# Four-layer attention kernel, one core: gated layers may start beside the layer that shares their memory, order of steps replaced

## Time and profile before

| | |
|---|---|
| median of 3 runs | 2008.59 us |
| the profiled execution | 2009.47 us, its span from first to last instruction 2007.7 us |
| PE, share of the span | 98% |
| DVE | 74% |
| ACT | 58% |
| POOL | 35% |
| DMA | 104.5 MB, mean 52 GB/s |
| TensorE's granted clock | full in all 40 slices |

### The profile page before, as it was taken

The page is one execution under the profiler, slowest core; times in us unless marked ns, Lnnn a source line. Parts: engine busy times, 40 slices in busy tenths (PEclk is TensorE's granted clock), DMA queues, the critical chain, the costliest instruction groups (busy, mean ns, idle before and its releaser), DMA issues.

```text
span 2007.7 us, 41814 instructions
## 1 busy us (share of the span) xinstructions
PE 1960.4 (98%) x15876; PEld 1257.5 (63%) x15876; DVE 1491.6 (74%) x4779; ACT 1155.5 (58%) x2602; POOL 711.1 (35%) x897
## 2 busy tenths in 40 slices
PE   8999999999999999999999999999999999999997
PEld 6666655666665666656666566755666566676566
DVE  8986667766878768868779687796787966856535
ACT  1554765575637766376644757367573676627642
POOL 6322325242433333333324334234153342313321
PEclk9999999999999999999999999999999999999999
DMA  4001211111211121112211112111120111202200
GB/s 171 2 2 43 71 64 61 56 64 35 69 33 50 64 59 46 55 36 74 59 38 45 54 56 63 39 59 54 46 70 30 62 54 39 66 27 72 71 16 7
DMA packets 33381, 104.52 MB, mean 52 GB/s; under 512 B 3360, under 2 KB 13728, under 8 KB 33056
## 3 DMA queue, kind: packets, MB, share of 16 engines
q1 hardware_dynamic: 30880, 99.76, 15.1%
q0 software_dynamic: 2304, 2.10, 0.9%
HBM read 95.56 MB, written 6.29 MB: 51 GB/s over the span
## 4 chain that ended last, share of the span: by engine, by line
PE 66%; DVE 21%; ACT 7%; issue 2%; POOL 1%; ACTq 0%; DVEq 0%; POOLq 0%
PE ps L981 18%; PE ps L1773 9%; PE ps L1755 9%; PE ps L1763 8%; PE ps L1527 6%; DVE probs L1474 4%; DVE ps L1374 3%; PE ps L1715 3%; PE ps L1624 3%; ACT PTc L1226 3%; PE ps L1703 3%; PE ps L1610 3%; PE ps L1681 2%; PE ps L1586 2%; ACT probs L1270 2%
## 5 line engine op out<-in xcount | busy, mean ns | idle before, releaser
L1162 POOL TENSOR_SCALAR probs<-probs,rtotal 128x512 f32<-128x512 f32 x512 | 347.6, 698 | 538.7 <-DVE rtotal L1483 538.1
L1270 ACT ACTIVATE probs<-probs,peak 128x512 f32<-128x512 f32 x512 | 365.0, 714 | 184.6 <-DVE peak L1479 184.0
L1474 DVE CUSTOM_DVE_ANT_0 probs<-ps,band 128x512 f32<-128x512 f32 x512 | 332.6, 687 | 79.3 <-PE ps L1755 78.9
L1279 ACT ACTIVATE PT<-ps 128x512 f32<-128x512 f32 x512 | 265.2, 620 | 24.7 <-PE ps L1763 24.7
L1763 PE MATMUL ps<-ident,probs 128*128 128x128 f32 x2048 | 250.7, 275 | 1.6 <-POOL probs L1162 1.4
L1763 PEld LDWEIGHTS ps<-ident,probs 128*128 128x128 f32 x2048 | 225.3, 141 | 42.7 <-issue 28.5
L1374 DVE CUSTOM_DVE_ANT_0 ps<-ps,later 128x512 f32<-128x512 f32 (+3 forms) x512 | 233.2, 527 | 17.1 <-PE ps L1586 16.1
L1755 PE MATMUL ps<-KT,QT 64*128 64x512 f32 x1024 | 242.9, 606 | 1.0 <-DVE QT L1463 0.6
L1773 PE MATMUL ps<-PT,Vb 128*64 128x512 f32 x1024 | 238.5, 601 | 0.0
L981 PE MATMUL ps<-xnT,wb 128*128 128x512 f32 x512 | 235.5, 600 | 0.9 <-ACT xnT L1189 0.6
L1226 ACT ACTIVATE PTc<-ps 128x384 f32<-128x384 f32 (+1 forms) x384 | 168.1, 550 | 62.4 <-PE ps L1610 61.2
(11 more groups left out here) (166 smaller groups left out, 3277.3 us busy)
## 6 DMA issues: line engine op xcount, KB each, us to landing
band<-in_band SPq DMA_DIRECT2D x64, 896.0 KB, 4.6
wb<-in_w_b SPq DMA_DIRECT2D x64, 384.0 KB, 3.1
x<-in_x SPq DMA_DIRECT2D x16, 256.0 KB, 3.7
out<-x SPq DMA_DIRECT2D x16, 256.0 KB, 2.1
cos<-in_cos SPq DMA_DIRECT2D x8, 256.0 KB, 2.6
sin<-in_sin SPq DMA_DIRECT2D x8, 256.0 KB, 2.9
wob<-in_wo_b SPq DMA_DIRECT2D x1, 1024.0 KB, 9.1
wqk<-in_wqk_a SPq DMA_DIRECT2D x1, 512.0 KB, 6.0
```

What stands on the lines that cost most here:

```text
L1162: last = g.tensor_scalar(unit, unit, rtotal[:, r % 8, e:e + 1], 1.0, ALU.mult, ALU.mult)
L1270: last = a.activation(unit, unit, ACT.Exp, bias=peak[:, r % 8, e:e + 1], accum_out=total[:, r % 8, e:e + 1])
L1279: a.activation(PT[:, k % 2, e, :, tile_of(q)], bank(now, name).rearrange("p (k n) -> p k n", k=NT), ACT.Copy).then_inc(act_read, 1)
L1474: v.tensor_tensor_reduce(out=probs[:, (r + LENT) % ROWS_HELD, e, :], in0=bank(now, name), in1=band[:, k % 2, e, lo:lo + T], scale=1.0, sca ...
```

## The change

Four things change.

1. In `whole()` the two gated layers no longer follow the whole layer ahead in their home. `held_back` adds conditions to single steps instead. Layer 3 of s-1 may start `f_ln` after the causal layer's last `c_p2`; its `f_part` and `f_gather` still wait for `c_y`. Layer 1 of s+1 may start `f_ln` after layer 3's last `f_p2`; `f_part` follows layer 3's last `f_vb`, `f_rank` its last `f_va`, `f_gather` and `f_spread` its `f_add`. In the last pass (s = 7) the old rule stands.
2. The early phase's tiles move inside the home to places that are free by then: `logit_junk`, `gate_row`, `above`, `tie` over `gHI` and `gLO`, `xn_lo` over the second half of `PTf`; in layer 3 one more set, `gated_last`, lies over the causal layer's `HI`.
3. Semaphore waits that this needs are added: on DVE ahead of the logits (for `c_p2` or `f_p2`), on ACT in `f_part` of layer 3 (for `c_y`), on POOL in `f_part` of layer 1 (for `f_vb`).
4. Every value of `PLACE` is replaced, in all 210 rows of the table; `CYCLE` and the costs in `WORK` stay.

No operation of the computation is added or left out.

```diff
-    ("cycle", "c_y"): [-896, -3188],
...
-    ("cycle", "f_ln"): [-120],
...
-    ("cycle3", "f_add"): [5190],
...
-    ("cycle3", "f_ln"): [2230],
...
-    ("cycle3", "f_sc"): [5404],
...
+    ("cycle", "c_y"): [-920, -2849],
...
+    ("cycle", "f_ln"): [-238],
...
+    ("cycle3", "f_add"): [5413],
...
+    ("cycle3", "f_ln"): [4142],
...
+    ("cycle3", "f_sc"): [5796],
...
+def held_back(layer, behind):
+
+    return [(x, a, b + behind.get(x.kind, [])) for x, a, b in layer]
...
-            side = add(ffn_steps(s - 1, 3), left, turned + side)
+            if turned:
+                last_p2 = [Step("c_p2", s + 1, 0, 3, 2)]
+                side = add(held_back(ffn_steps(s - 1, 3), {"f_part": turned, "f_gather": turned, "f_turn": turned}), left, last_p2)
+            else:
+                side = add(ffn_steps(s - 1, 3), left, side)
             if s + 1 < B:
-                side = add(ffn_steps(s + 1, 1), turned, side)
+                done = {"f_part": [Step("f_vb", s - 1, 3, 1)], "f_rank": [Step("f_va", s - 1, 3, 1)],
+                        "f_gather": side, "f_spread": side}
+                side = add(held_back(ffn_steps(s + 1, 1), done), turned, [Step("f_p2", s - 1, 3, 3)])
...
-                         part("xn_lo", 1024, [P, NT, D], F32R), part("pick", 3072, [P, NT, CAP], F32R),
-                         part("logit_junk", 4096, [P, NT, D]), part("gate_row", 5120, [P, T]),
+                         part("xn_lo", 5120, [P, NT, D], F32R), part("pick", 3072, [P, NT, CAP], F32R),
+                         part("logit_junk", 1024, [P, NT, D]), part("gate_row", 1024, [P, T]),
...
+                                if l == 1 and s >= 2:
+                                    at_least(pool, dve_full, plan.unit(Step("f_vb", s - 2, 3, 1), now))
...
+                            if l == 3 and s + 2 < B:
+                                at_least(act, dve_full, plan.unit(Step("c_y", s + 2, 0, 1), now))
...
+                            if kind == "f_ln" and l == 3 and s + 2 < B:
+                                at_least(dve, act_full, last_unit(Step("c_p2", s + 2, 0, 3, 2), now))
+                            if kind == "f_ln" and l == 1 and s >= 2:
+                                at_least(dve, act_full, last_unit(Step("f_p2", s - 2, 3, 3), now))
```

More of the change, by code:

```diff
@@ L314 @@
[L314 to L327, removed]
@@ L328 @@
[L328 to L341, removed]
@@ L397 @@
-    ("last1", "f_hk"): [16566],
-    ("last1", "f_hm"): [12587, 16487],
-    ("last1", "f_idx"): [28848],
-    ("last1", "f_k"): [16502],
-    ("last1", "f_ln"): [29156],
-    ("last1", "f_m"): [15479, 24859],
-    ("last1", "f_mk"): [13382],
-    ("last1", "f_p1"): [13899, 13347, 15820, 13912],
-    ("last1", "f_p2"): [14402, 16479, 15277, 15555],
-    ("last1", "f_part"): [15919],
-    ("last1", "f_q"): [24858],
-    ("last1", "f_rank"): [15078],
-    ("last1", "f_row"): [13349],
-    ("last1", "f_rq"): [29156],
@@ L426 @@
-    ("last2", "f_p1"): [20538, 19976, 20663, 20764],
-    ("last2", "f_p2"): [20786, 20935, 20608, 20468],
-    ("last2", "f_part"): [18279],
-    ("last2", "f_q"): [20057],
-    ("last2", "f_rank"): [20308],
-    ("last2", "f_row"): [20165],
-    ("last2", "f_rq"): [-859],
-    ("last2", "f_sc"): [23696],
-    ("last2", "f_v"): [20786],
-    ("last2", "f_va"): [21047, 21532],
-    ("last2", "f_vb"): [15227, 17058],
-    ("last2", "f_xq"): [20405],
+    ("cycle", "b_k"): [823, 329, 785, 911, 1209, 1703, 2405, 2804],
@@ new lines @@
+    ("cycle", "f_k"): [195],
+    ("cycle", "f_ln"): [-238],
+    ("cycle", "f_m"): [320, 364],
+    ("cycle", "f_o"): [612],
+    ("cycle", "f_p1"): [272, 273, 299, 327],
+    ("cycle", "f_p2"): [344, 357, 272, -226],
+    ("cycle", "f_part"): [-356],
+    ("cycle", "f_q"): [198],
+    ("cycle", "f_rank"): [77],
+    ("cycle", "f_row"): [-30],
+    ("cycle", "f_rq"): [231],
+    ("cycle", "f_spread"): [225],
+    ("cycle", "f_v"): [271],
+    ("cycle", "f_va"): [406, 546],
+    ("cycle", "f_vb"): [152, -630],
@@ new lines @@
+    ("cycle3", "f_part"): [3793],
+    ("cycle3", "f_q"): [5082],
+    ("cycle3", "f_rank"): [4832],
+    ("cycle3", "f_row"): [4569],
+    ("cycle3", "f_rq"): [3074],
+    ("cycle3", "f_sc"): [5796],
+    ("cycle3", "f_v"): [5085],
+    ("cycle3", "f_va"): [5505, 5635],
+    ("cycle3", "f_vb"): [5095, 5471],
+    ("cycle3", "f_xq"): [3583],
+    ("first", "b_k"): [-499, 948, -411, 218, 1567, 2212, 3083, 2202],
+    ("first", "b_ln"): [2790],
+    ("first", "b_nrm"): [1568, 1572, 622, 1089, 206, 1709, 698, 377, 1317, 1576, 2189, 2190, 2222, 2188, 1994, 2216,
+        3004, 1566, 923, -1603, 3029, 215, 1361, 2270, 1466, 2531, 2638, 2332, 329, 2199, 3415, 3302],
@@ new lines @@
+    ("first0", "c_xq"): [-10, 355],
+    ("first0", "c_xt"): [8233],
+    ("first0", "c_y"): [902, -1196],
+    ("first0", "f_gate"): [344],
+    ("first0", "f_gather"): [1165],
+    ("first0", "f_hk"): [155],
+    ("first0", "f_hm"): [-200, 1237],
+    ("first0", "f_k"): [330],
+    ("first0", "f_ln"): [603],
+    ("first0", "f_m"): [1241, 1460],
+    ("first0", "f_o"): [1498],
+    ("first0", "f_p1"): [1221, 1171, 1282, 1238],
+    ("first0", "f_p2"): [-201, 1369, -1220, 493],
+    ("first0", "f_part"): [987],
@@ new lines @@
+    ("first0", "f_q"): [15],
+    ("first0", "f_rank"): [1071],
+    ("first0", "f_row"): [971],
+    ("first0", "f_rq"): [270],
+    ("first0", "f_spread"): [1370],
+    ("first0", "f_v"): [332],
+    ("first0", "f_va"): [1461, 1232],
+    ("first0", "f_vb"): [-212, -336],
+    ("first0", "f_xq"): [1033],
+    ("first0", "f_y"): [1958, 2332],
+    ("first1", "c_dk"): [418, 595],
+    ("first1", "c_dq"): [376, 519],
+    ("first1", "c_hk"): [276, 809],
+    ("first1", "c_hm"): [269, -266],
+    ("first1", "c_k"): [274, 300],
@@ new lines @@
+    ("first1", "c_xt"): [-1338],
+    ("first1", "c_y"): [2334, 3645],
+    ("first1", "f_gate"): [785],
+    ("first1", "f_gather"): [1490],
+    ("first1", "f_hk"): [1301],
+    ("first1", "f_hm"): [1270, 1389],
+    ("first1", "f_k"): [1715],
+    ("first1", "f_ln"): [-588],
+    ("first1", "f_m"): [2144, 2432],
+    ("first1", "f_o"): [3104],
+    ("first1", "f_p1"): [1300, 1583, 1968, 2203],
+    ("first1", "f_p2"): [2210, 2562, 2333, 2916],
+    ("first1", "f_part"): [-268],
+    ("first1", "f_q"): [1719],
@@ new lines @@
+    ("first1", "f_rank"): [1215],
+    ("first1", "f_row"): [-3058],
+    ("first1", "f_rq"): [1094],
+    ("first1", "f_spread"): [3082],
+    ("first1", "f_v"): [1807],
+    ("first1", "f_va"): [2726, 2334],
+    ("first1", "f_vb"): [2806, 2973],
+    ("first1", "f_xq"): [1871],
+    ("first1", "f_y"): [3140, 407],
+    ("last", "b_k"): [20360, 20417, 20604, 20802, 19009, 23530, 20508, 21299],
+    ("last", "b_ln"): [20070],
+    ("last", "b_nrm"): [20421, 20566, 20314, 20067, 20139, 20314, 20529, 20145, 21280, 21071, 16408, 16201, 21809,
+        21528, 21367, 21570, 21470, 18111, 20239, 21466, 21812, 19552, 21367, 20829, 20855, 20956, 20854, 20868, 20794,
+        19689, 20134, 19927],
@@ new lines @@
+    ("last1", "f_gather"): [19916],
+    ("last1", "f_hk"): [20716],
+    ("last1", "f_hm"): [15147, 19060],
+    ("last1", "f_idx"): [20758],
+    ("last1", "f_k"): [15693],
+    ("last1", "f_ln"): [19782],
+    ("last1", "f_m"): [19633, 20046],
+    ("last1", "f_mk"): [19815],
+    ("last1", "f_p1"): [19339, 15661, 19791, 19404],
+    ("last1", "f_p2"): [19632, 19846, 15660, 14371],
+    ("last1", "f_part"): [19867],
+    ("last1", "f_q"): [18648],
+    ("last1", "f_rank"): [20028],
+    ("last1", "f_row"): [19782],
@@ new lines @@
+    ("last1", "f_rq"): [20781],
+    ("last1", "f_sc"): [19649],
+    ("last1", "f_v"): [19501],
+    ("last1", "f_va"): [19867, 18797],
+    ("last1", "f_vb"): [20186, 20758],
+    ("last1", "f_xq"): [20717],
+    ("last2", "f_add"): [21027],
+    ("last2", "f_gate"): [17951],
+    ("last2", "f_gather"): [20570],
+    ("last2", "f_hk"): [18798],
+    ("last2", "f_hm"): [20868, 21212],
+    ("last2", "f_idx"): [20962],
+    ("last2", "f_k"): [20625],
+    ("last2", "f_ln"): [20263],
+    ("last2", "f_m"): [20957, 20956],
@@ L438 @@
+    ("last2", "f_mk"): [20197],
+    ("last2", "f_p1"): [19952, 20855, 20867, 20934],
+    ("last2", "f_p2"): [21045, 6262, 20564, 20148],
+    ("last2", "f_part"): [19818],
+    ("last2", "f_q"): [20631],
+    ("last2", "f_rank"): [20434],
+    ("last2", "f_row"): [20389],
+    ("last2", "f_rq"): [19783],
+    ("last2", "f_sc"): [23294],
+    ("last2", "f_v"): [20631],
+    ("last2", "f_va"): [21352, 22231],
+    ("last2", "f_vb"): [19872, 20103],
+    ("last2", "f_xq"): [20738],
 }
@@ L858, in hybrid_kernel, with behind_causal @@
         gated = [gated_memory(i) for i in range(2)]
+        def behind_causal(i):
+            return gated[i]._replace(
+                xn_lo=over(side[i], 1024, f"xn_lo{i}b", [P, NT, D], F32R), logit_junk=over(side[i], 2048, f"logit_junk{i}b", [P, NT, D]),
```

(5 more changed lines are left out.)

251 lines of the change are left out of this document (96 added, 155 removed).

## The result

The changed kernel takes 2080.4 us (median of 4 runs, 2078.71 to 2080.82), against 2008.71 us for the kernel before on the same chip: a ratio of 1.0354, 95% interval 1.0341 to 1.0367. It is slower by 72 us, far outside the range given.

What follows compares the result with a forecast made beforehand. The home, not an engine, was taken as what the change loosens. Waits -10, shape changes -3, new waits and port meetings +4, ends 0 sum to -9 us: forecast 2000.0 us, range 1986 to 2012.

Steps and rivals of the forecast that it cites:

- Moved, layer 1: Where layer 1 follows layer 3: early phase could start near 733, gather near 750 after `f_add`'s landing, 15 us earlier.
- Removed and added work: Whole kernel: no computation added or removed, only semaphore waits on DVE, ACT and POOL, free where their work is done.
- Queues passed: POOL's 1/sqrt goes ahead of `f_add`'s DMAs, the SP queue's x load goes out earlier: zero for both.
- The home as the thing loosened: Repeated middle: the home, not an engine, is loosened, gaining about 25 us of slack per 240 us period.
- the 10 forecast: Where layer 3 follows the causal layer: gather could start near 927, 10 us earlier, with the early phase before `c_y`.
- What the slack is worth: Middle: waits give -10 us, half of the 20 us listed; ceiling 24 us, floor nothing; shape changes -3 us.
- shape changes: PE's changes of tile shape in the middle: 3 fewer of 95 per period, at 0.15 us each, -3 us.
- The term of 0 for the ends: Head and end of the run: only the replaced keys act there; bounds -10 and +8 us, taken as 0.
- The one on the slower side that named a wait in a queue: DVE waits ahead of the logits for `c_p2` or `f_p2`, holding up score-bank readers: 2018 us, chance 0.12.
- signs listed for a wrong forecast: Period unchanged or longer, DVE idle before the logits, POOL's subtractions or scalings longer, or time changed at the ends.
- 1970: Extreme of the larger-gain rival: all middle idle gone, fewer shape runs, ends give 8; case put at 1989, chance 0.17.
- The rival of port meetings: Early phase's DVE work meets POOL at the shared port: two meetings a period, +10 us, 2006 to 2015, chance 0.08.

Runs made afterwards that it cites:

- e1: Changed kernel with tile `of` moved off `xgT`, and ACT's wait for the landed DMAs moved from the gather to `f_sc` and `f_o`: 2006.33 us.
- e5: e1 with the three lines of ACT's wait for the landed DMAs put back in the gather: 2080.29 us.
- e4: Changed kernel with the `PLACE` table of before, so the new structure with the old keys: 2051.56 us.
- e3: Kernel before the change with tile `of` moved off `xgT`: 2009.30 us.

## Why the prediction was wrong

**The step that failed** is in "Moved, layer 1" and in "Removed and added work". I wrote that the gather then "waits for the `f_add` issued to 745.5 and its landing" and counted this as a time at which the gather could start at the earliest. I didn't ask who waits: it is not PE but ACT, in the middle of its queue, with the biased layer's reads behind. And I looked for costs only in the waits that the diff adds, while the loss stands at a wait that was in the kernel before and had never been felt, with 20 us between the DMAs and the gather. So the sum has no term for it. It measured 13 us on ACT and 8.9 us on PE, six times, and e1 and e5 show that this wait alone carries the 72 us.

Nor does `f_add` keep its place. I let POOL issue the DMAs as early as in the kernel before (743.90 + 1.56), 14 us behind the start of the last `f_p2` at 731.46. In the changed kernel the second one is issued at 786.97, 39 us behind it. Most of this is the new order, which puts layer 3's output matmuls (`f_sc`, tile `wof`) later: 775.10 - 747.81 = 27.3 us behind the last `f_p2` in place of 738.24 - 731.46 = 6.8. The rest is POOL's queue, with six pairs of scalings, 8.0 us, ahead of `f_add`. The rows of the changed kernel, then that of the kernel before:

```profile
747.81 0.33 PE L1731 MATMUL ps<-gM,sel 32*128 32x256 f32 x4
...
775.10 1.97 PE L1555 MATMUL ps<-wof,OTf 128*128 128x256 f32 x8
```

```profile
738.24 1.94 PE L1527 MATMUL ps<-wof,OTf 128*128 128x256 f32 x8
```

"Queues passed" spoke of one instruction that goes ahead of `f_add` on POOL and not of what `f_add` itself now stands behind.

Why the list has it so can be read in the code: in the walk `f_gather` only *follows* `f_add`, which sets an order and no time, and `f_add` is costed as two POOL instructions, without a landing. The keys do the rest. `f_sc`, ahead of `f_add`, has 5796 - 5640 = 156, which the prediction itself worked out, and the gather has -181, so the gather goes out as soon as `f_add` is placed (distance 1, six times of six). The distance was 35; of it 30 entries come from `f_add` standing later behind the last `f_p2` (43 entries in place of 13) and 4 from the gather standing earlier (44 in place of 48). With the old keys the distance stays 35 under the new rule too (e4), and no wait for the DMAs is left there. So it is the new keys that bring the two together, and the new rule that lets them.

**The home as the thing loosened:** right in kind, half the size. With the wait gone (e1) the early phases run early. `c_y` to gather of layer 3 takes 701.32 - 689.18 = 12.1 us in place of 937.16 - 917.77 = 19.4, 7 us of the 10 forecast. From the last `f_p2` to the gather of layer 1 it is 765.35 - 736.45 = 28.9 us in place of 765.57 - 731.46 = 34.1, 5 us of the 15. Rows of e1:

```profile
689.18 3.62 PE L1558 MATMUL ps<-woa,Xf 128*128 128x256 f32 x16
...
736.45 0.32 PE L1734 MATMUL ps<-gM,sel 32*128 32x256 f32 x4
...
765.35 0.47 PE L1001 MATMUL ps<-pick,xn_hi 128*128 128x256 f32 x1
```

**What the slack is worth:** its split was wrong, its size too large. I expected 10 us from waits and 3 us from shape changes. In e1 the middle's idle time has risen to 28.2 us (1750.00 - 1721.76 below) from 23.9:

```profile
0.00:175.00 175.00, 163.00 (x1691) 112.11 (x1692) 151.92 (x504) 73.10 (x150) 68.18 (x86) 0.99 0.14 50
175.00:1925.00 1750.00, 1721.76 (x13571) 1094.57 (x13571) 1320.59 (x4183) 1063.37 (x2415) 625.13 (x803) 1.00 0.17 54
```

Over one period, from e1 and from the kernel before, PE's busy time falls by 2.1 us and its idle time rises by 1.1:

```profile
701.32:940.40 239.08, 234.57 (x1918) 149.37 (x1917) 188.56 (x599) 144.00 (x325) 87.05 (x110) 1.00 0.17 53
712.69:952.74 240.05, 236.64 (x1917) 149.16 (x1918) 186.81 (x597) 144.10 (x325) 88.28 (x110) 1.00 0.17 53
```

PE's waits, then, gave nothing back. What fits the fall is the changes of tile shape, 84 in this period of e1's timeline and 95 before: an estimate of 11 x 0.15 us = 1.65 us. No run tests it by itself.

Not every period gains, and the 3.6 us between the two profiled spans are made up in three places. The first gather of layer 3 is at 459.52 us in place of 457.05, a loss of 2.5. From there to its sixth gather e1 takes 1657.66 - 459.52 = 1198.14 us in place of 1658.12 - 457.05 = 1201.07, a gain of 2.9 over five periods. From there to the end it takes 346.4 in place of 349.6, a gain of 3.1. The term of 0 for the ends came out near (-0.6 in all) because two changes of some 3 us cancel, which is luck.

**Rivals.** The one on the slower side that named a wait in a queue had the right kind and the wrong place: DVE ahead of the logits, at 1.5 us a period. That wait shows in no list of the changed kernel, of e1 or of e4. What e4 shows is its neighbour, DVE waiting for POOL's 1/sqrt ahead of the normalising, with 4.1 us of PE behind it. A wait of 13 us on ACT costs 13 less the 4 that PE has work for, and a little for the clock. None of the signs listed for a wrong forecast named ACT or the DMAs.

Two slips in the working bear on nothing above. Half of the distance from the forecast to 1970 is 1985; 1989 is half of the distance from the time before. And the earlier trace rows has the clock at 0.98 behind 1925 us, so it is not quite full throughout.

The rival of port meetings had a real mechanism and too high a price. In e1 the meeting has left layer 3's first scores for layer 1's. Its timeline there, POOL, DVE, PE:

```profile
776.61 3.07 POOL L1162 TENSOR_TENSOR gLO<-gLOf,gHI 128x512 fp32r<-128x512 f32 x2
777.58 3.19 DVE L1387 SCALAR_TENSOR_TENSOR gX<-gDq,sides,gX 128x1024 fp32r<-128x1024 f32 x1
780.83 0.39 PE L1712 MATMUL ps<-gLO,gX 32*128 32x256 f32 x4 [1.12 <-DVE gX L1387]
```

The multiply-add takes 3.19 us beside POOL, where the earlier trace rows has 1.27, and PE waits 1.12 us for it. The rule of the Trainium skill that the prediction weighed ("SBUF — State Buffer", "Who interferes with whom") agrees with this row too, with 3.19 against 1.27 us. The meeting is not one of the early phase, though, where the prediction looked for it. But in the whole of e1's middle such waits are 7.5 us in 7, about one a period, where the kernel before had about one of 0.8 us a period at layer 3's scores; the difference is 7.5 - 4.8 = 2.7 us over the run, not the 10 of that rival.

## What to carry to other kernels

When work between a producer and a consumer is moved away, look up every wait that the two already have with one another, and name for each the engine that will stand, what is queued behind it there, and what the producer now stands behind in its own queue: a wait that is never felt is covered by distance, and the distance is what such a change removes. A planner that orders steps must know as a time, not only as an order, whatever ends with a DMA's landing. And a tile laid over a DMA's source can cost a stall: moving it changed nothing in the kernel before (e3) and took away a loss of 72 us in the changed one (e1).

## What was unexpected in the hardware

A stall of PE costs more than its length. Per period e1 and the changed kernel differ by 251.69 - 239.08 = 12.6 us, while the stall is 8.8 us. Where the rest goes can be read between the same matmuls. In e1 they stand so:

```profile
769.28 1.99 PE L1786 MATMUL ps<-KT,QT 64*128 64x512 f32 x8
771.20 1.99 PE L1001 MATMUL ps<-xgT,wkf 128*128 128x256 f32 x8
773.03 1.89 PE L1001 MATMUL ps<-xgT,wqf 128*128 128x256 f32 x8
```

`f_k` takes 773.03 - 771.20 = 1.83 us there and 3.23 in the changed kernel at the lower clock: 1.4 us. From the start of the 8 matmuls of the scores (6 and 2 in the changed kernel) to that of `f_k` it is 771.20 - 769.28 = 1.9 us in e1 and 793.43 - 780.67 = 12.8 in the changed kernel, 10.8 more; beyond the 8.8 of the stall that leaves 2.1 us. In these the lower clock and a next wait of PE are not told apart: the weight loads of `f_k` stand 1.50 us for ACT's reads of the transposes.

```profile
793.43 3.00 PEld L1001 LDWEIGHTS ps<-xgT,wkf 128*128 128x128 f32 x8 [1.50 <-ACT PT L1303]
```

So 1.4 us of the 3.8 beyond the stall are the clock's; how much of the rest is, stays open. Behind the shorter stall of e4, 4.1 us, the clock falls too: in the stretch around it the granted clock averages 0.83.

```profile
668.00:680.00 12.00, 7.89 (x35) 2.76 (x32) 8.22 (x32) 5.29 (x15) 3.24 (x5) 0.83 0.00 0
```

The indirect adding DMA, of 128 KB, takes POOL 1.6 us per issue, and from the start of the issue to the landing it is 3.8 us (median of 16). The Trainium skill ("DMA: Bandwidth & Descriptors", "Anatomy of one DMA — SWDGE (gpsimd) path") fits a DMA issued by POOL by 2.0 us plus its bytes over 436 GB/s, an estimate of 2.3 us here. The measured 3.8 decides. Counted from the end of POOL's instruction it is 3.8 - 1.6 = 2.2 us, so the difference is about as long as that instruction.
